# Four-layer graph network with a Mamba last layer: staggered sums in layer 2, doubled step sizes computed in place, and GpSimd's products moved to steps 0, 1 and 4 of eight

## The reference, cut to what matters

```python
def _L2_gnn_ref(h, adj, weight, a_l, a_r, b):
    x = h @ weight
    scores = (x @ a_l)[:, None] + (x @ a_r)[None, :]
    attn = jnp.where(adj != 0, jnp.exp(leaky_relu(scores, 0.2)), 0.0)
    denom = jnp.maximum(attn.sum(axis=-1, keepdims=True), 1e-12)
    return attn / denom @ x + b

def _L3_gnn_ref(x, adj, gcn_w, gcn_b, ln_g, ln_b, ...):
    h = relu(adj @ x @ gcn_w + gcn_b)
    h = layernorm(h) * ln_g + ln_b
    return _mamba(h, ...)

def _mamba(h, w_in, conv_w, conv_b, w_xp, w_dt, b_dt, A_log, D_skip, w_out):
    xc, z = halves of h @ w_in                      # 256 channels each
    u = silu(causal conv of xc over 4 taps + conv_b)
    dbc = u @ w_xp
    dt = softplus(dbc[:, :8] @ w_dt + b_dt)
    B, C = dbc[:, 8:24], dbc[:, 24:]                # 16 states
    dA = exp(dt[:, :, None] * -exp(A_log)[None])
    dBu = dt[:, :, None] * B[:, None, :] * u[:, :, None]
    # per row of x: hst = dA * hst + dBu ; ys = hst @ C
    y = (ys + u * D_skip) * silu(z)
    return y @ w_out

x = layernorm(x + _L2_gnn_ref(x, adj, ...))
x = layernorm(x + _L3_gnn_ref(x, adj, ...))
```

## Time and profile before

| what | us |
|---|---|
| median of 3 runs (932.04 to 934.73) | 933.14 |
| the profiled execution, whole | 937.67 |
| its span, first to last instruction | 935.8 |
| TensorE busy | 824.3 (88%) |
| VectorE busy | 690.8 (74%) |
| ScalarE busy | 508.2 (54%) |
| GpSimd busy | 231.0 (25%) |
| mean granted TensorE clock | 0.932 |

### The profile page before, as it was taken

The page is one execution under the profiler, slowest core; times in us unless marked ns, Lnnn a source line. Parts: engine busy times, 40 slices in busy tenths (PEclk is TensorE's granted clock), DMA queues, the critical chain, the costliest instruction groups (busy, mean ns, idle before and its releaser), DMA issues. The chain is left out here.

```text
span 935.8 us, 11963 instructions
## 1 busy us (share of the span) xinstructions
PE 824.3 (88%) x4196; PEld 523.5 (56%) x4196; DVE 690.8 (74%) x975; ACT 508.2 (54%) x802; POOL 231.0 (25%) x132
## 2 busy tenths in 40 slices
PE   6999988999999999999599989979579889787755
PEld 6755537888888888854354569954223333231211
DVE  2986889999999999427843148851177888989897
ACT  2654537777877777535220147522457666666461
POOL 2000000000000000000020010001368887877992
PEclk9999998999999999999699979989779999897777
DMA  8589975221122021069100000000432715517210
GB/s 278 189 314 330 360 283 224 91 91 44 46 90 90 0 90 45 1 278 423 47 1 0 1 0 1 1 23 1 115 90 58 159 34 139 123 35 164 64 45 11
DMA packets 39360, 102.42 MB, mean 109 GB/s; under 512 B 6122, under 2 KB 11132, under 8 KB 32788
## 3 DMA queue, kind: packets, MB, share of 16 engines
q1 hardware_dynamic: 38116, 100.55, 32.6%
q10 hardware_dynamic: 1200, 1.32, 0.5%
HBM read 75.33 MB, written 18.14 MB: 100 GB/s over the span
## 5 line engine op out<-in xcount | busy, mean ns | idle before, releaser
L1752 PE MATMUL PS<-big 128*128 128x256 f32 x768 | 194.4, 385 | 3.9 <-ACT big L1582 3.8
L221 PE MATMUL PS<-ident,big 128*128 128x128 f32 x1123 | 158.5, 281 | 22.4 <-DMA big<-in_L_gnn_weight 7.3
L221 PEld LDWEIGHTS PS<-ident,big 128*128 128x128 f32 x1123 | 136.9, 146 | 47.2 <-issue 21.3
L445 POOL TENSOR_TENSOR big<-big 128x1024 f32<-128x1024 f32 x64 | 149.9, 2352 | 20.4 <-DVE big L1318 9.2
L1752 PEld LDWEIGHTS PS<-big 128*128 128x128 f32 x768 | 133.9, 191 | 22.1 <-ACT big L1582 7.6
L1582 ACT ACTIVATE big<-PS 128x512 f32<-128x512 f32 x192 | 105.0, 598 | 58.3 <-PE PS L221 57.3
L1318 DVE TENSOR_TENSOR_SCAN big<-PS,stripes,big 128x512 f32<-128x512 f32 x96 | 116.3, 1260 | 3.6 <-POOL big L445 3.1
L404 POOL MEMSET big<- 128x16 f32 x1 | 0.1, 127 | 465.2 <-DVE big L1120 465.2
L1951 DVE SCALAR_TENSOR_TENSOR big<-big,rz 128x2048 f32<-128x2048 f32 x48 | 112.7, 2350 | 0.9
L1929 DVE CUSTOM_DVE_ANT_0 big<-big 128x2048 f32<-128x2048 bf16 x48 | 109.7, 2289 | 0.1
L688 ACT ACTIVATE PS<-big,stripes 128x512 f32<-128x512 f32 x128 | 86.2, 686 | 40.9 <-DVE big L1318 40.4
(11 more groups left out here) (207 smaller groups left out, 1002.0 us busy)
## 6 DMA issues: line engine op xcount, KB each, us to landing
big<-in_adj SPq DMA_DIRECT2D x16, 2048.0 KB, 9.0
big<-at_dram SPq DMA_DIRECT2D x4, 4096.0 KB, 27.3
at_dram<-big SPq DMA_DIRECT2D x3, 4096.0 KB, 16.6
big<-b_dram SPq DMA_DIRECT2D x32, 256.0 KB, 4.4
big<-big SPq DMA_DIRECT2D x24, 256.0 KB, 4.7
big<-b_dram SPq DMA_DIRECT2D x36, 128.0 KB, 4.0
at_dram<-big SPq DMA_DIRECT2D x1, 3072.0 KB, 18.8
big<-e_dram SPq DMA_DIRECT2D x3, 1024.0 KB, 6.8
```

What stands on the lines that cost most here:

```text
L221: return nc.tensor.transpose(PS[:, bank, col:col + P], src, ident[:])
L445: nc.gpsimd.tensor_tensor(dbu[k % 3], du2[c % 2][:, 2 * (n % 2):2 * (n % 2) + 2, :], bb[group % 2][:, pair_of(k) % 2, :].unsqueeze(1).to_b ...
L1752: m = nc.tensor.matmul(PS[:, 4 + k // 3, 0:256], hw[:, jt, h, :], qt[v % 4][:, 256 * c:256 * c + 256], start=(h == 0 and jt == 0), stop=(h ...
```

## The change

Layer 2: TensorE takes source tiles 0 to 12 as before, then waits for all factors and runs over the targets, with the last three source tiles inside, so that banks are complete one after the other. `after_layer2` takes its sums' banks in four parts instead of two.

Opening: `w_dt` is stored with each 64 channels twice (five small loads instead of three feed `w4_in`), so that `dt_product` of chunk 0 gives dt already doubled, as four products in banks 6, 7, 2, 3. For chunk 0 SP doubles `u` instead of dt and dt*u, GpSimd makes dt*u in place (`first_du`), and the ACT queue issues no transfers. `piece` and the first decays stand between the softplus parts.

Scan: `POOLS` goes from (1, 4, 6) to (0, 1, 4). `offset` (minus mean times inverse root) goes from DVE (line 1289) to ACT as a copy and four scalings. In a chunk's start TensorE takes `h_fill` and `out_product` one step earlier, ahead of the sums; the 8 convolution products lie 2, 3, 3 in steps 2 to 4 where they lay 1, 3, 4; `cuts` is evened; DVE's residual comes at step 2, not 3.

```diff
-        w_dt = wt[:, 11:13, :].rearrange("p a m -> p (a m)")
+        w_dt = wt[:, 9:13, :].rearrange("p a m -> p (a m)")
-        POOLS = (1, 4, 6)
+        POOLS = (0, 1, 4)
+        FIRST_DT = (6, 7, 2, 3)
...
+                if c == 0:
+                    for b in range(DI):
+                        sp.wait_ge(u_ready, b + 1)
+                        by_blocks(sp, u, du2[0], slice(b, b + 1), du2_in[b])
                 sp.wait_ge(dbc_ev, c + 1)
...
                     b_rows(c, 0)
-                    for b in range(DI):
-                        sp.wait_ge(du_ready, b + 1)
-                        by_blocks(sp, du, du2[0], slice(b, b + 1), du2_in[b])
                     sp.wait_ge(a_mm, 2)
...
+            def first_du(q):
+                pool.wait_ge(du2_in[q // 2], 64)
+                pool.wait_ge(dt_ready, dt_count(0, q))
+                nc.gpsimd.tensor_tensor(du2[0][:, q, :], dt2[0][:, q, :], du2[0][:, q, :], ALU.mult).then_inc(du_first, 1)
...
-            for b in range(DI):
-                make_du(0, b)
-            for k in range(3):
-                make_dbu(k)
+            for k in range(2):
+                for b in range(DI):
+                    first_du(2 * k + b)
+                make_dbu(k)
+            make_dbu(2)
...
+            def offset(offsets, root, count, first, done, nth):
+                cols = slice(first, first + 4)
+                nc.scalar.activation(offsets[:, cols], mv[:, cols, 0], ACT.Copy, scale=-1.0).then_inc(done, 1)
+                act.wait_ge(root, count)
+                act.wait_ge(done, 2 * nth - 1)
+                for i in range(first, first + 4):
+                    m = nc.scalar.activation(offsets[:, i:i + 1], offsets[:, i:i + 1], ACT.Copy, scale=rstd[:, i:i + 1])
+                m.then_inc(done, 1)
...
-            for jt in range(NT):
+            LAST = 3
+            for jt in range(NT - LAST):
...
+            pe.wait_ge(q2_ready, NT)
+            for it in range(NT):
+                for jt in range(NT - LAST, NT):
+                    m = weighted(jt, it)
+                if it % 3 == 2 or it == NT - 1:
+                    m.then_inc(l2_mm, 1)
...
-                    h_fill(c, 1)
-                elif n == 2:
                     if c >= 2:
                         pe.wait_ge(zg_ready, 3 * (c - 1))
-                    conv_part(c, 0, 0, range(0, 1))
+                    h_fill(c, 0)
+                elif n == 2:
+                    conv_part(c, 0, 0, range(0, 2))
                 elif n == 3:
-                    conv_part(c, 0, 0, range(1, 4))
-                elif n == 4:
+                    conv_part(c, 0, 0, range(2, 4))
                     if c >= 2:
                         pe.wait_ge(o_added, c - 1)
-                    conv_part(c, 1, 1, range(TAPS))
+                    conv_part(c, 1, 1, range(0, 1))
+                elif n == 4:
+                    conv_part(c, 1, 1, range(1, TAPS))
...
-                if c and n == 3:
+                if c and n == 2:
                     dve.wait_ge(o_mm, c)
```

More of the change, by code:

```diff
@@ L201, in gnn_program @@
         res_mm = sem("res_mm")
-        dt2_in, du2_in = [sem("dt2_in%d" % b) for b in range(DI)], [sem("du2_in%d" % b) for b in range(DI)]
+        dt2_in, du_first, du2_in = sem("dt2_in"), sem("du_first"), [sem("du2_in%d" % b) for b in range(DI)]
         dt_mm, sp_abs, sp_exp, sp_ln, dt_ready, du_ready = (sem("dt_mm"), sem("sp_abs"), sem("sp_exp"), sem("sp_ln"),
@@ L338, in later_loads @@
             sp.wait_ge(x_ready, 8)
-            sp.dma_start(w_dt[96:96 + DTR, :], t["L3_gnn_w_dt"]).then_inc(w4_in, 16)
-            sp.dma_start(w_dt[96 + DTR:97 + DTR, :], t["L3_gnn_b_dt"].rearrange("(o f) -> o f", o=1)).then_inc(w4_in, 16)
+            for s in range(2):
+                twice = w_dt.rearrange("p (q s r) -> p s q r", s=2, r=HALF)[:, s]
+                sp.dma_start(twice[96:96 + DTR], t["L3_gnn_w_dt"].rearrange("k (q r) -> k q r", r=HALF)).then_inc(w4_in, 16)
+                sp.dma_start(twice[96 + DTR:97 + DTR],
+                             t["L3_gnn_b_dt"].rearrange("(o q r) -> o q r", o=1, r=HALF)).then_inc(w4_in, 16)
             sp.wait_ge(x_ready, 12)
@@ L704, in later_act @@
             dbc_copy(0, 4)
-            for b in range(DI):
-                dt_abs(0, b, 6 + b)
-            for b in range(DI):
-                dt_log(0, b)
-                act.wait_ge(dt_ready, b + 1)
-                by_blocks(act, dt_, dt2[0], slice(b, b + 1), dt2_in[b])
-            for p in range(3):
-                piece(0, p, 4)
-            for j in range(3):
-                decay(j)
+            for q in range(3):
+                dt_abs(0, q, FIRST_DT[q])
+                dt_log(0, q)
+                piece(0, q, 4)
+                if q:
+                    decay(q - 1)
+            dt_abs(0, 3, FIRST_DT[3])
+            dt_log(0, 3)
+            decay(2)
             a_copy(1, 1)
@@ L760, in later_act @@
                     exp_and_log()
-                if c and n == 4:
+                if c and n == 3:
                     inverse_root(o_var, c, 4 * (c - 1), 4, o_log, o_root)
+                    offset(bj, o_root, c, 4 * (c - 1), o_off, c)
                 elif c and n == 6:
@@ L894, in later_pe, with weighted @@
             pe.wait_ge(ones_col, 1)
-            for jt in range(NT):
+            def weighted(jt, it):
+                return nc.tensor.matmul(sums(it, slice(0, P + 1)), q2[jt % 4][:, it * P:(it + 1) * P], x2[:, jt, :],
+                                        start=(jt == 0 and it % 3 == 0), stop=(jt == NT - 1), skip_group_check=True)
+            LAST = 3
+            for jt in range(NT - LAST):
                 pe.wait_ge(q2_ready, jt + 1)
@@ L898, in later_pe @@
                 for it in range(NT):
[L899 to L905 removed]
+                    m = weighted(jt, it)
+                m.then_inc(q2_used, 1)
                 if jt == 0:
@@ L1025, in later_pe @@
             a_part(1, 1, 7, 8)
-            for b in range(DI):
-                dt_product(0, b, 6 + b)
+            for q in range(4):
+                dt_product(0, q, FIRST_DT[q])
             pe.wait_ge(sel_ready, 6)
+            a_part(1, 1, 8, 10)
             take_off(0, 0, 4)
-            a_part(1, 1, 8, 9)
+            a_part(1, 1, 10, 12)
             take_off(0, 1, 4)
-            a_part(1, 1, 9, NT)
+            a_part(1, 1, 12, NT)
             gcn(1, 1)
@@ L1283, in h_spread @@
                 spread_of(bank_tiles(bank), 4 * c, 4, h_var)
-            def offset(offsets, root, count, first, done):
-                dve.wait_ge(root, count)
-                cols = slice(first, first + 4)
-                nc.vector.scalar_tensor_tensor(offsets[:, cols], mv[:, cols, 0], -1.0, rstd[:, cols], ALU.mult,
-                                               ALU.mult).then_inc(done, 1)
             def h_rescale(c, bank):
@@ L1344, in later_dve @@
             h_rescale(0, 2)
-            for b in range(DI):
-                softplus(0, b, 6 + b)
+            for q in range(4):
+                softplus(0, q, FIRST_DT[q])
             scan(0)
-            h_spread(1, 1)
             for k in range(STEPS):
@@ L1366, in later_dve @@
                     spread_of(xo[c - 1], tile, 4, o_var)
-                if c and n == 5:
-                    offset(bj, o_root, c, 4 * (c - 1), o_off)
-                if c < NCH - 1:
-                    if n == 0:
-                        offset(dj, h_root, c + 2, 4 * (c + 1), h_off)
-                    elif n == 8 or n == 9:
-                        softplus(c + 1, n - 8, 0)
+                if c < NCH - 1 and (n == 8 or n == 9):
+                    softplus(c + 1, n - 8, 0)
                 if c < NCH - 2 and n == 15:
```

123 lines of the change are left out of this document (66 added, 57 removed).

## The result

The changed kernel takes **922.6 us** (median of 4 runs, 921.9 to 924.1), the kernel before in the same session 933.2 (932.0 to 934.7). The ratio is 0.988, interval 0.9856 to 0.9907: faster, by 10.6 us between the medians, clear of the noise. I had predicted 921.2, range 914 to 929. The profiled execution took 922.90 around a span of 921.1.

The account below looks back on a forecast made before the run. It took TensorE's order to hold chunks 0 and 1, DVE and POOL together chunk 3, and one dependent chain ahead of the scan. -3.0 - 6.0 + 0.8 - 3.7 = -11.9 from a median of 933.14 gave 921.2 us, range 914 to 929.

Parts of the forecast that it names:

- The forecast's own case: Whole kernel: layer 2, opening and chunk 3 gain, chunks 1 and 2 lose slightly; -11.9 us to 921.2; chance 0.50.
- Rival 1: More is kept: DVE, not PE, sets chunks 0 to 2; 912.6 us; chance 0.17.
- Rival 3: Layer 2 gains nothing, its new 3.1 us wait eats the staggering and chunk 3 gains 2.5; 925.4 us; chance 0.12.
- Rival 4: Slower: PE stays at half clock through each chunk's opening; at 17 us of it 938.0 us; chance 0.06.
- Rival 2: The opening's lead is lost to PE idling and staying at half clock, gain only 2; 925.2 us; chance 0.15.
- B: Opening, counted at chunk 1's start: scans start earlier, part of the lead is lost; -6.0 us, bounds -9 and -2.
- A: End of layer 2: less waiting for X, adjacency products at full clock; -3.0 us, between -4.5 and -0.5.
- the wait of 1.0 that I put at the spread of step 6: Chunk 0 after step 5: PE waits 1.0 us there, with no sums to fill it.
- a sign that I was wrong: The forecast is wrong if POOL is what DVE waits for; no size given.
- my second sign of being wrong: The forecast is wrong if PE's clock stays at half through an opening; 5.9 us at half was expected.
- C: Chunks 1 and 2: the new order nets 0 in chunk 2, costs 0.8 in chunk 1; +0.8 us, bounds -8 and +4.
- D: Chunk 3: DVE's waits for POOL end, less 0.9 and 0.8 for PE; -3.7 us, bounds -5.4 and -1.5.

Follow-up runs that it names:

- b_l2open: The kernel before with only the new end of layer 2 and the new opening, old order in the chunks and POOLS (1, 4, 6); 923.6 us.
- a_warm: The changed kernel with idle fill products on PE ahead of the transposes of chunks 1 to 3 (seven, then five each); 915.5 us.
- b_pools: The kernel before with only POOLS changed from (1, 4, 6) to (0, 1, 4); 936.6 us.
- b_orderpools: The kernel before with only the new order inside the chunks and POOLS (0, 1, 4); 933.9 us.

## Why the prediction was right, step by step

**The forecast's own case came true**: TensorE's order holds chunks 0 to 2, the lead comes from layer 2 and the opening, and part of it is lost in chunk 0. Time 922.6 for 921.2. Rival 1 wanted chunks 1 and 2 shorter by 5, they are by 1.0. Rival 3 wanted nothing from layer 2, it gives 2.6. Rival 4 needed more half clock than there was. Rival 2 is the nearest of them: it wanted B at -2, it is -4.3. Of the four parts three were off by 1.3 to 1.8 us, two one way and one the other; that the total is off by only 1.4 is in part luck.

**A, -3.0 forecast, -2.6 measured** (32.9 to 30.3), inside [-4.5, -0.5]. Every step stands: the last 48 products begin at 609.2 on before's axis (forecast 609.2), DVE's first quarter at 615.3 (614.8), the products end at 621.9 (620.0 to 621.7), the adjacency products run at clock 1.00. Taking the middle between full and half clock was right in kind: the clock was at half for part of the 48 here (12.63 us), and at full in three of the other profiles (10.99), where A comes out at -4.2. The rule that I weighed ("TensorE: Matmul & The Clock Gate", section "What's actually happening", in the Trainium skill), that the moment of switching isn't tied to the kernel's start and varies, agrees with these two numbers for one and the same code.

**B, -6.0 forecast, -4.3 measured** (133.5 to 126.7, less A), inside [-9, -2]. The mis-sized term is the clock in the opening. I had PE at full clock there, since before has it up to the end of its dt products:

```profile
658.33 1.98 PE L965 MATMUL PS<-big,wt 9*128 9x512 f32 x4
```

Now eight such records take 4.78, and the clock was at half from 653.9 to 660.7. Piece 1 ended at 665.3 on before's axis and scan 0 began at 671.2, where the forecast with A's 3.0 taken off was 661.9 and 668. b_l2open, without that fall, shows what it costs: 3.1 us from the adjacency products to scan 0. Of the lead, 7.0 were left at step 5 (forecast 9.0): from `h_scale`'s end to the spread it took 15.6 us for my 16.6, so 1.0 of the 3 us came back. From there to the chunk's end 2.7 were lost (forecast 3.0), but the agreement is luck in one term: the wait of 1.0 that I put at the spread of step 6 isn't there, and in its place DVE's waits at the products of steps 10 and 13 grow by 1.0 together, to 3.00 us at step 13. POOL is what DVE waits for at scans 1, 3 and 4 (1.1 to 1.6 each), which I had named as a sign that I was wrong; but it still waits 3.32 for PE's spread of step 5 behind them, so they cost nothing. The half clock of chunk 1's opening, 671 to 681, which goes with my second sign of being wrong, was in the forecast with 5.9 us of PE's work and holds 3.4; the fill of a_warm, which removes it and its like in chunks 1 and 2, gains about 7 in all.

**C, +0.8 forecast, -1.0 measured**: +0.3 in chunk 1 (forecast +0.8), -1.3 in chunk 2 (0). DVE's waits there are for the spreads of steps 2 (1.1 and 1.7 us) and 5 (2.0 and 2.0), as said, but the longest of chunk 1 is at step 13, which I hadn't, behind six adjacency records on PE:

```profile
784.87 2.84 PE L956 MATMUL PS<-big 128*128 128x512 f32 x6
...
788.02 1.22 DVE L1370 TENSOR_TENSOR big<-PS,big 128x1024 f32<-128x1024 f32 x1 [2.64 <-issue]
```

The sign "within 1 us of its old length" failed for chunk 2. The mis-sized term is the path to the spreads: in chunk 2 `h_scale` starts 8.6 us behind the chunk's start (11.0 before, forecast 9.8), and the spread of step 5 comes 1.2 us earlier than before, where I had it 0.7 later. What else I didn't see is that the new order alone costs 3.7 and only the move of step 0 to POOL pays for it; I costed the two together, which is why C came out near.

**D, -3.7 forecast, -2.4 measured**: the stretch to product 63 is 56.3 long, not 54 to 55. DVE waits for POOL only for scan 48 itself (1.63), and no longer behind it. The 0.8 that I took off for the spread of step 50 didn't come. In its place came a wait that I hadn't in the sum. ACT and DVE in chunk 3:

```profile
886.12 0.60 ACT L326 ACTIVATE big<-PS 128x512 f32<-128x512 f32 x1 [3.17 <-PE PS L989]
...
887.92 1.28 ACT L639 ACT_TABLE_LOAD   x1
...
890.35 1.28 ACT L709 ACT_TABLE_LOAD   x1
...
892.37 2.46 DVE L1359 TENSOR_TENSOR_SCAN big<-PS,stripes,big 128x512 f32<-128x512 f32 x2 [2.02 <-ACT PS L722]
```

ACT waits 3.17 us for PE's product of the gate, copies it, and then the gate's silu wants another table, 1.28 us to and 1.28 back, with the decays of the next scan behind it. The two loads are as long before (at 901.68 and 904.11), so they are not what is new. Before, DVE came to the same scan (the second of step 58) 39.0 us into the chunk; now it comes at 35.0, which is 4.0 earlier, but ACT's first decay behind the loads comes at 36.3 for 37.8, only 1.5 earlier. How much of it is PE's part a_warm shows, where that product takes 1.12 us at full clock for 2.02 here:

```profile
875.92 0.60 ACT L326 ACTIVATE big<-PS 128x512 f32<-128x512 f32 x1 [2.14 <-PE PS L989]
...
882.18 2.46 DVE L1361 TENSOR_TENSOR_SCAN big<-PS,stripes,big 128x512 f32<-128x512 f32 x2 [0.99 <-ACT PS L722]
```

ACT's wait is 1.0 shorter, and so is DVE's; this is the 1.0 that a_warm's chunk 3 gains. DVE's wait is also in b_pools and b_orderpools (1.35 and 2.00) and not in b_l2open.
